# A new order for merging the steps of seven lanes: the table made anew from measured step lengths

## The reference, cut to what matters

```python
x = x + 0.5 * ffn(layernorm(x))      # half 0
x = x + mamba_and_mlp(layernorm(x))
x = x + 0.5 * ffn(layernorm(x))      # half 1, the same weights
# inside ffn:
x = x + attn(x)                      # layernorm, conv, q/k/v, rope, causal softmax, projection
h = layernorm(x); e = argmax(h @ router_w)
x = x + (silu(h @ gate[e]) * (h @ value[e])) @ expert_proj[e]
```

## Time and profile before

| | |
|---|---|
| median of three runs | 1715.63 us (1712.78 to 1719.43) |
| profiled execution, from its first to its last instruction | 1727.8 us |
| PE busy | 1426.8 us (83%) |
| DVE busy | 1173.5 us (68%) |
| ACT busy | 800.8 us (46%) |
| POOL busy | 400.0 us (23%) |

### The profile page before, as it was taken

The page is one execution under the profiler, slowest core; times in us unless marked ns, Lnnn a source line. Parts: engine busy times, 40 slices in busy tenths (PEclk is TensorE's granted clock), DMA queues, the critical chain, the costliest instruction groups (busy, mean ns, idle before and its releaser), DMA issues.

```text
span 1727.8 us, 30410 instructions
## 1 busy us (share of the span) xinstructions
PE 1426.8 (83%) x11328; PEld 747.2 (43%) x11328; DVE 1173.5 (68%) x2803; ACT 800.8 (46%) x1266; POOL 400.0 (23%) x406
## 2 busy tenths in 40 slices
PE   1567779979978989898998989899899888796946
PEld 1223444544433545344454545354455444443423
DVE  4556585687685787668767779778786677565622
ACT  1243443644544565354553566455555454263522
POOL 3000132232332131412123031513133214211120
PEclk8687878979988999898897999899999899797978
DMA  6220200303020030122101221121202103002110
GB/s 188 36 33 25 48 1 18 55 1 53 20 31 24 8 59 19 36 38 45 27 19 34 40 47 20 48 41 31 38 13 53 49 1 55 23 2 54 31 35 23
DMA packets 75807, 61.43 MB, mean 36 GB/s; under 512 B 6800, under 2 KB 71824, under 8 KB 75664
## 3 DMA queue, kind: packets, MB, share of 16 engines
q1 hardware_dynamic: 70704, 50.31, 14.8%
q0 software_dynamic: 4096, 8.40, 1.6%
q10 hardware_dynamic: 864, 0.79, 0.4%
HBM read 19.23 MB, written 14.55 MB: 20 GB/s over the span
## 4 chain that ended last, share of the span: by engine, by line
PE 42%; DVE 14%; issue 6%; SPq 3%; DMA 3%; ACT 3%; POOL 2%; POOLq 0%; DVEq 0%; ACTq 0%
PE wring L747 7%; PE wring L554 5%; PE obank L600 5%; PE wring L752 4%; DVE mx L1307 4%; PE aring L615 4%; SPq L463 3%; PE aring L657 3%; PE aring L640 2%; PE wring L760 2%; PE aring L580 2%; DMA stq<-shiftT 2%; DVE conv L1443 1%; PE wring L862 1%; PE wring L766 1%
## 5 line engine op out<-in xcount | busy, mean ns | idle before, releaser
L943 ACT ACTIVATE prob_mem<-aring 128x1024 f32<-128x1024 f32 x320 | 324.9, 1021 | 185.5 <-PE aring L657 172.0
L1307 DVE TENSOR_REDUCE mx<-aring 128x2 f32<-128x1024 f32 (+2 forms) x384 | 317.6, 861 | 128.8 <-PE aring L640 117.6
L615 PE MATMUL aring<-ramps,spots 64*128 64x128 bf16 (+1 forms) x2560 | 179.9, 220 | 88.3 <-DVE mx L1307 26.4
L747 PE MATMUL wring<-wv,hb 128*128 x448 | 238.1, 637 | 7.8 <-ACT hb L980 4.9
L615 PEld LDWEIGHTS aring<-ramps,spots 64*128 64x128 bf16 x2560 | 84.5, 97 | 307.6 <-issue 193.1
L600 PE MATMUL obank<-prob_mem,vx 128*9 128x512 f32 (+3 forms) x2048 | 193.3, 477 | 15.0 <-ACT prob_mem L943 9.1
L1418 DVE SCALAR_TENSOR_TENSOR yv<-yv,wring 128x512 f32<-128x512 f32 x112 | 76.6, 684 | 99.4 <-ACT yv L985 98.5
L657 PE MATMUL aring<-stq,stk 50*128 50x384 bf16 (+3 forms) x1024 | 135.0, 323 | 0.0
L640 PE MATMUL aring<-stk,stq 48*128 48x512 bf16 (+3 forms) x1024 | 134.4, 324 | 0.0
L752 PEld LDWEIGHTS wring<-ep,yaT 128*128 128x128 f32 x896 | 112.7, 194 | 44.1 <-issue 43.6
L752 PE MATMUL wring<-ep,yaT 128*128 x896 | 126.9, 285 | 5.7 <-ACT yaT L877 3.5
(11 more groups left out here) (212 smaller groups left out, 2377.3 us busy)
## 6 DMA issues: line engine op xcount, KB each, us to landing
hb<-hd SPq DMA_DIRECT2D x16, 448.0 KB
stq<-high SPq DMA_DIRECT2D x96, 64.0 KB
stk<-high SPq DMA_DIRECT2D x90, 64.0 KB
stq<-mid SPq DMA_DIRECT2D x64, 64.0 KB
od<-ob SPq DMA_DIRECT2D x16, 256.0 KB, 2.3
stk<-mid SPq DMA_DIRECT2D x60, 64.0 KB
od<-ob SPq DMA_DIRECT2D x16, 192.0 KB, 2.0
x<-in_x SPq DMA_DIRECT2D x8, 256.0 KB, 2.8
```

The costliest lines, as they stand in the source:

```text
L615: pe.matmul(dst, spots[rows, 2 * by_key + part, :], ramp, start=(part == 0), stop=False, skip_group_check=True)
L747: last = pe.matmul(ring[:], hTd[:, u * P:(u + 1) * P], wv[:, expert[u], o:o + DFF], start=True, stop=True)
L943: act.activation(prob_mem[:, k], ring[:], ACT.Exp, scale=float(HD) ** -0.5).then_inc(freed, 1)
L1307: last = dve.tensor_reduce(mx[:, j, h0 + q:h0 + q + 3:2], ring[:, :, c:c + w], AX_X, ALU.max)
```

## The change

`ORDER` has a new content. It is still a string of 1952 digits with the same number of each digit (768 of lane 1, 480 of 4, 352 of 3, 144 of 0, 128 of 2, 64 of 5, 16 of 6), made from the measured mean length of each step. All other lines stay, and so do the order within each lane and every instruction with its waits, except that `fills` gives the steps other turns in the two rings. The diff, with the first and the last lines of the table:

```diff
@@ -156,24 +156,24 @@
 ORDER = (
-    "00000000000011111111001110111111101111111111110111111111001111101111121122202112212111100116110114114444440444"
...
-    "14144414114101411414411411444410141110111114202020424242402021116114145114445511444411114444141514411141141111"
-    "4441411411144114115114411441455111111122222522264444444444444444444444544444444444555"
+    "00000000000111111110111111101111110111111101011111111110011110010111111212121212021621121011011110411441444414"
...
+    "10411141041414111444115010011410101411424242442442111214111215264411414114144114111411414411411114114115111114"
+    "4114151141511611452424242424425242444444444444444444444444444444444445445555445544444"
 )
```

More of the change, by code:

```diff
@@ L174 @@
-    "14014354131144331313410151003153333311033313101335311111211221231213211212311313613131333311134011441144114414"
-    "14144414114101411414411411444410141110111114202020424242402021116114145114445511444114411444141514411141141111"
-    "4441411411144114115114411441455111111122222522264444444444444444444444544444444555"
+    "00000000000111111110111111101111110111111101011111111110011110010111111212121212021621121011011110411441444414"
+    "44144441144104514044444144441441104511111011115111533033333333131131131112123312121123312332133123600331303311"
@@ new lines @@
+    "33101343144411334144444114404344444411434131544444354114434115133110331135331131113313033331331111331111313121"
+    "13212312332331123021133231310361331033034041144444101311404304411434114144444144444141130445143410134105331133"
+    "05533311310333133331331113331111113111101303231123211331131213331210332113321336211311310113114111114411311143"
+    "41144044111404301151414114211442411444424441241214402451142354112331130331651133113111031011143311013344411033"
+    "11444114411144411443434341114443111413331311424144211442451233411324511321125113312115363113311313311113411013"
@@ new lines @@
+    "31044110344113404044010144114444410414454004111054430111431411142141244123412112330320301012551311311632113111"
+    "31133013313113441041144131141134411411444114344111434133411453344313111314211424444111252454311341131213313321"
+    "13211513113211113110103110141136411141043414400014034100444114430341011414111321134214442444121551420344211544"
+    "21142311303111301516311301113114341014133311144114311131444441031344131144131141341114211324442144413431144334"
+    "11331123451134315251331113112311211133315211311111311103614410140444304300041040410145344144014140441441114241"
@@ new lines @@
+    "42411445234412112430350331153123323112331331133131361310113401114414444413114111431410414111434410403314044111"
+    "40131130111153141341323411140421130112114341121323113210121311114331216513511111311141341100441411434115314441"
+    "43111432144211444424441524211544442114426114425343311331113101541344443304104131333333113401404444441301134111"
+    "04511434411411434413143313031031333131133313313112321314123231423132142311231133361134111341014151414411511101"
+    "10411141041414111444115010011410101411424242442442111214111215264411414114144114111411414411114114115111111114"
@@ L177 @@
+    "4114151141511611452424242424425242444444444444444444444444444444444445555445544444"
 )
```

## The result

The changed kernel takes 1599.84 us (median of four runs, 1585.4 to 1600.82) against 1714.2 us in the same comparison: a ratio of 0.9325, 95% interval [0.9274, 0.9375], 114 us less. The forecast was 1684 with a range down to 1642. The direction was right, the size was not: the gain is 3.7 times the forecast of 31.

What follows compares the result with a forecast made beforehand. It took TensorE's 300 us of standing still, in a strict step order, as the bound. End -18.5 and middle -12.8 summed to -31.3: a span of 1696, a median of 1684 us, range 1642 to 1713.

Steps and rivals of the forecast that it cites:

- End: Last B stage, start of C15, what that costs and the clock at the end: together -18.5 us.
- The last B stage: Chain of the last B stage: E14 steps cover its 20.9 us of waits, 5.3 left, 15.6 saved.
- The wait at C15: C15's first maximum waits 9.5 us for the last stacked row; more steps ahead leave 3.4, saving 6.1.
- C15 gave back: C15 loses about 8 us of E14 work that filled its waits; 5 us given back (0 to 8).
- Middle, links without cover: Dependent step pairs outside the last row with no PE step between fall from ten to two: 7.5 us saved.
- shift rows behind stacks: Middle: SP issues stacks ahead of shift rows, five PE waits cost 17.7 us; 6 left, 11.7 saved.
- The sum of the middle: Uncovered links 7.5 plus shift rows 11.7, two thirds kept for gather and `aring` losses: -12.8 us.
- The shift transposes: Middle, cover between a group's last maximum and its shift: between -4 and +2.4 us, taken as 0.
- Clock at the end: E15's first gate and value took 3.77 us against 1.98 later; 1.8 us saved when PE stays busy (0 to 5).
- Larger gain through the clock: Rival, chance 0.20: fewer holes lift the mean clock from 0.886 to 0.91, matmuls shrink 37 us; -65, 1650 us.
- Slower: a table without slack: Rival, chance 0.13: mean-length merging leaves some 600 links without slack, one late input delays all lanes; 1744 or 1725 us.
- What would show it: Signs, right: `hb` wait under 4 us, C15's under 5, shift rows' under 8; wrong: VectorE waits at a combine.

Runs made afterwards that it cites:

- e7: Old table with a step of another lane moved between each of nine uncovered pairs of dependent B and E steps; 1711.1 us, ratio 0.9994.
- e3: Old table with eight `high` and `mid` stack steps, at seven shifts, moved behind the shift they stood ahead of; 1721.8 us, ratio 1.0068.
- e9: Old table with one to three steps of lanes E or M pulled ahead of each of 29 TensorE waits; 1711.9 us, ratio 1.0008.
- e13: Every step stays in its old table's pass but stands within it as in the new table; 1679.9 us, ratio 0.9812 against the old kernel.
- e16: New placement within old passes, but the 51 steps crossing an earlier border than C13's first maximum in their new pass; 1634.4 us, ratio 0.9594.
- e4: Old table with 262 idle matmuls of constants added ahead of 61 TensorE waits of 0.8 us or more; 1678.6 us, ratio 0.9787.
- e11: New table with only the rank of pass 6 moved directly behind its logits, ahead of pass 5's gather; 1612.4 us, ratio 0.9413 against the old kernel.
- e14: Old table with the 84 steps that change pass moved to their new pass, old order kept within passes; 1780.5 us, ratio 1.0404.
- e6: Old table with only lane F's steps moved to their new-table places among lane C's steps; 1830.2 us, ratio 1.0680.
- e5: New table with 155 idle matmuls of constants added ahead of 34 TensorE waits of 0.8 us or more; 1569.2 us, ratio 0.9143 against the old kernel.
- e2: Old table up to C14's first maximum, from there the remaining steps in the new table's order; 1682.8 us, ratio 0.9833.
- e12: New table with seven lane B steps put directly behind their predecessors, but pass 5's gather kept ahead of pass 6's rank; 1606.5 us, ratio 0.9385.

## Why the prediction was wrong

*End: right.* Forecast -18.5, the trace shows 148.3 to 131.1, -17.2. The last B stage left 28.40 - 23.10 = 5.3 us of idle PE, the forecast's very number; but 1.7 of it are waits of the covering experts' own `down` (L752), which the forecast hadn't, so that the agreement to the tenth is luck. The wait at C15 is 2.8 (forecast 3.4). C15 gave back as it said: 64.0 us for 66.4, with its idle time risen from 5.0 to 9.1. E15's first gate is at the full clock.

*Middle, links without cover* and *shift rows behind stacks*: right in the trace, 9.2 and 10.6 us for 7.5 and 11.7; but e7, and e3 as far as it tells, gained nothing from taking these waits away on the old table. The trace says where PE waits, not what it would gain without that wait: in e3, e7 and e9 other waits grew by as much.

*The sum of the middle: the step that failed.* It took the waits of two kinds, held every other row of the middle at its old value, and kept two thirds, -12.8. The trace shows -58.7 of idle time there. Of what it set off against the gain, the waits for `aring` buffers rose by 4.1 us (20.7 to 24.8), and no early gather held PE up; the 10.1 us on stacked rows it hadn't foreseen. The shift transposes, put at 0, gave 8.7, and some twenty rows that it held fixed gave the rest. Covering many waits at once wasn't enough for that: e9 moved 47.5 us of cover by hand and got nothing, and in e13 to e16 parts of the new order gave parts of the gain or a loss. What in the order as a whole makes these rows fall together stays open.

*Clock at the end: the second step that failed.* It counted 1.8 us for one gate. PE's busy time fell 52.7 us in the profiles, some 37 by the medians, all in the middle (0.91 to 0.94). e4 prices the clock on the old order at 31 to 36. The rival *Larger gain through the clock* had this mechanism and nearly this size ("37 us"), but not the fewer waits; it ended at 1650. Its argument against itself held by count, the middle has 37 waits of 1 to 3 us where it had 50, and the clock rose all the same. That every hole that is filled pays a second time, as it also says, no run shows: e4 put 79 us of matmuls into 61 waits and gained 31 to 36.

*Slower: a table without slack* did not come. That one late input holds up other lanes is real: e11's chain passes through three engines, and mixtures of the two orders cost 4.0% (e14) and 6.8% (e6). But these are orders that don't fit together; no run varied the slack alone.

*What would show it:* the waits on `hb` (0.8 us) and ahead of C15 (2.8) and on the shift rows (7.9 in all, limit 8) were as named for a right forecast, the first two as signs of the end alone; PE's busy time, which was to fall "a little", fell 52.7 us. VectorE's wait at the combines, named as a wrong sign, is 19.1 us in all for 14.5, 15.1 of it at the last combine of all.

What stays open: which of the measured lengths brought the better order, and how much of the middle each engine's queue contributes. Orders were exchanged only for all engines at once.

## What to carry to other kernels

In a static interleaving of lanes don't price a new order by the waits that it removes one by one. Compare it as a whole, and check for each engine's queue which step passes which: waits taken away one by one gave nothing in three trials, and one scatter ahead of one gather made PE wait 14 us. The price by single waits held only at the end of the run, where the work lent to them was priced too. Where the main engine has many waits of about 1 us and more, price its clock as well. Matmuls of constants in the waits of 0.8 us and more took 2% off either table, and the new table with them, 1569.2 us, is the fastest version found.

## What the runs showed of the hardware

Much of this kernel, whose PE waits often and for a few us, runs at the lower clock. A mean of 0.886 between 1.2 and 2.4 GHz means 2 x (1 - 0.886) = 23% of 1728 us at the lower clock, 394 us; in the new table it is 262, in e4 225, in e5 158. By the clock records PE was busy in 296 of the 394 and in 197 of the 262. The same order had this differ between two profiles: C1 to C13 took 1186 us of busy PE in the old kernel's and 1166 in e2's.

GpSimd's fourth scatter in a row started 6.1 us after the third in e11, where the others follow at 0.30. In the new table and in e12, with the gather ahead of the scatters, no such gap shows at that place. Shorter ones, 1.9 to 3.9 us and always ahead of the fourth of four, stand at four of the 32 scatters and gathers of the old trace and at two of the new. The profile names no releaser for it ("issue"), and what holds the queue there wasn't tested.
